# Splitting the shared expert weights earlier and running six shared units, not four, among the block projections

## Time and profile before

| what | value |
|---|---|
| median of 3 runs | 399.27 us (399.08 to 399.86) |
| the profiled execution | 399.35 us |
| its span, first to last instruction | 397.5 us |
| PE busy | 360.5 us (91%) |
| DVE busy | 310.6 us (78%) |
| POOL busy | 236.7 us (60%) |
| ACT busy | 185.4 us (47%) |

### The profile page before, as it was taken

One profiled execution on the slowest core, in us unless ns is written; L12 is line 12 of the kernel. 1 busy time (PEld: TensorE's weight loads), 2 busy tenths in 40 slices (PEclk: granted clock), 3 DMA queues, 4 the chain that ended last, 5 costly groups with the idle time before them and its releaser, 6 DMA issues.

```text
span 397.5 us, 12279 instructions
## 1 busy us (share of the span) xinstructions
PE 360.5 (91%) x4303; PEld 312.3 (79%) x4303; DVE 310.6 (78%) x846; ACT 185.4 (47%) x434; POOL 236.7 (60%) x200
## 2 busy tenths in 40 slices
PE   0166998998999999999999999999999999999993
PEld 0064675665767777777789999999999999999992
DVE  5988888978989999999967788666666666666663
ACT  2667842767344677777665444222222232222220
POOL 1555902157787773343106999188866767667676
PEclk9996999999999999999999999999999999999998
DMA  8954520001154797758663656666565555653333
GB/s 294 297 133 108 127 89 2 0 23 57 50 121 120 172 193 152 166 136 160 134 124 84 194 183 126 138 84 71 65 73 56 62 60 61 61 60 30 30 34 32
DMA packets 99157, 41.34 MB, mean 104 GB/s; under 512 B 73888, under 2 KB 92704, under 8 KB 99104
## 3 DMA queue, kind: packets, MB, share of 16 engines
q1 hardware_dynamic: 87408, 31.82, 35.0%
q0 software_dynamic: 11264, 8.69, 16.5%
q10 hardware_dynamic: 432, 0.11, 0.2%
HBM read 10.94 MB, written 12.88 MB: 60 GB/s over the span
## 4 chain that ended last, share of the span: by engine, by line
PE 81%; DVE 10%; POOL 3%; DMA 2%; issue 2%; ACT 1%; DVEq 0%; POOLq 0%; ACTq 0%
PE pY L863 18%; PE pY L696 12%; PE pAB L839 9%; PE pAB L837 9%; PE pAB L838 9%; PE pAB L684 6%; PE pAB L686 6%; PE pAB L685 6%; PE pV L708 4%; DVE hot L1201 2%; DVE hbuf L1291 1%; DMA base<-in_x 1%; POOL units L1109 1%; DMA xT<-hot 1%; POOL rows L1101 1%
## 5 line engine op out<-in xcount | busy, mean ns | idle before, releaser
L1154 POOL DMA_INDIRECT out_dram<-xT,rows x64 | 98.9, 1545 | 46.5 <-DVE xT L1653 26.6
L1145 POOL DMA_INDIRECT sorted_rows<-rows,slot x64 | 70.5, 1102 | 51.6 <-DVE hbuf L1291 38.5
L1088 ACT ACTIVATE units<-pAB 128x512 f32<-128x512 f32 x78 | 46.4, 594 | 108.9 <-PE pAB L839 93.1
L837 PE MATMUL pAB<-rows,wsp 128*128 128x128 f16 x512 | 87.6, 219 | 0.0
L838 PE MATMUL pAB<-rows,wsp 128*128 128x128 f16 x512 | 87.6, 219 | 0.0
L839 PE MATMUL pAB<-rows,wsp 128*128 128x128 f16 x512 | 87.6, 219 | 0.0
L1591 DVE SCALAR_TENSOR_TENSOR hbuf<-pAB,units 128x512 f32<-128x512 f32 x78 | 53.6, 687 | 37.6 <-PE pAB L839 37.2
L863 PE MATMUL pY<-wsp,hbuf 128*128 (+1 forms) x620 | 78.7, 279 | 0.5 <-issue 0.4
L863 PEld LDWEIGHTS pY<-wsp,hbuf 128*128 128x128 f32 x620 | 72.7, 192 | 0.8 <-issue 0.8
L696 PEld LDWEIGHTS pY<-wsp,hbuf 128*128 128x128 f32 x512 | 66.7, 191 | 8.3
L696 PE MATMUL pY<-wsp,hbuf 128*128 128x128 f32 x512 | 68.0, 276 | 0.0
(11 more groups left out here) (166 smaller groups left out, 588.4 us busy)
## 6 DMA issues: line engine op xcount, KB each, us to landing
base<-in_x SPq DMA_DIRECT2D x8, 512.0 KB, 7.4
out_dram<-base SPq DMA_DIRECT2D x16, 256.0 KB, 2.5
wraw<-in_wall SPq DMA_DIRECT2D x10, 256.0 KB, 3.1
rows<-hot SPq DMA_DIRECT2D x8, 256.0 KB, 2.7
proj<-sorted_rows SPq DMA_DIRECT2D x27, 68.5 KB, 1.9
wsp<-in_wall SPq DMA_DIRECT2D x10, 128.0 KB
sorted_rows<-rows,slot POOLq DMA_INDIRECT x64, 2.5
out_dram<-xT,rows POOLq DMA_INDIRECT x64, 3.4
```

The lines of the kernel that those rows point to most:

```text
L837: pe.matmul(o, hi, x(0), start=True, stop=False)
L1088: nc.scalar.activation(silu[:, q % 2, 0:job.cols], pAB[:, 2 * (q % 2), 0:job.cols], ACT.Silu, scale=1 / (XS * WS)).then_inc(d_silu, 1)
L1145: pool.indirect_dma_start(sorted_rows, bass.IndirectOffsetOnAxis(ap=slot[:, t:t + 1].bitcast(U32), axis=0), rows[:, t, :], None, bounds_ch ...
L1154: pool.indirect_dma_start(out_rows, bass.IndirectOffsetOnAxis(ap=meta[:, t, DEST - CW:DEST - CW + 1].bitcast(U32), axis=0), yt[:, t], None ...
```

## The change

The split of the shared weights moves to earlier steps; six units in place of four run among the projections; the units at which PE and ACT do their parts of the routing are renumbered; on DVE two calls of `shared_unit()` between routing pieces go, the column counts move behind the logit maximum, two softmax pieces are joined, one call is added behind the clip, and the attention tables move behind unit 25.

```diff
-HIGH_AT, LOW_AT = (5, 8), (8, 10)
+HIGH_AT, LOW_AT = (3, 5), (4, 6)
...
-EARLY = 4
-EARLY_AT = {6: 0, 8: 1, 10: 2, 11: 3}
-GAP_UNIT, COLUMN_UNIT, STEP_UNIT, PLACE_UNIT = 7, 10, 10, 12
-SEG_UNIT, TAB_UNIT, TABLE_UNIT, SIDES_UNIT = 15, 18, 20, 26
-LOGIT_UNIT, ABS_UNIT, WHOLE_UNIT, SIGN_UNIT = 16, 14, 19, 20
-SELECT_UNITS = (5, 6, 12, 13)
+EARLY = 6
+EARLY_AT = {4: 0, 6: 1, 8: 2, 9: 3, 11: 4, 12: 5}
+GAP_UNIT, COLUMN_UNIT, STEP_UNIT, PLACE_UNIT = 9, 11, 12, 14
+SEG_UNIT, TAB_UNIT, TABLE_UNIT, SIDES_UNIT = 17, 20, 24, 28
+LOGIT_UNIT, ABS_UNIT, WHOLE_UNIT, SIGN_UNIT = 18, 15, 20, 21
+SELECT_UNITS = (7, 8, 10, 11)
...
-                pe.wait_ge(w_split, e // 2 % 2 + 1)
+                pe.wait_ge(w_split, e // 2 % NSH + 1)
...
             ins.then_inc(paired_ready, 1)
-            shared_unit()
 
             dve.wait_ge(gap_tanh, 1)
...
-            shared_unit()
-
-            assert unit[0] == COLUMN_UNIT
-            dve.wait_ge(column_done, 1)
...
             then(v.tensor_tensor(wmax[:, 0], halves4[:, :, :, 0], halves4[:, :, :, 1], ALU.max))
             shared_unit()
 
+            assert unit[0] > COLUMN_UNIT
+            dve.wait_ge(column_done, 1)
...
+            shared_unit()
+
             idx3 = idx.rearrange("p (t k) -> p t k", k=HP)
             v.tensor_scalar(offsets, offsets, 127.5, -128.0, ALU.min, ALU.max).then_inc(clipped, 1)
             shared_unit()
 
+            shared_unit()
...
             then(v.reciprocal(quad_recip, sum_quads))
-            shared_unit()
...
+            def tables():
+
+                dve.wait_ge(table_done, 1)
...
-                if n == 0:
+                if n == 1:
+                    tables()
+                if n == 2:
                     spread_out()
-                if n == 1:
+                if n == 3:
                     extra_table()
```

More of the change, by code:

```diff
@@ L1381, in _ @@
             shared_unit()
+            assert unit[0] > COLUMN_UNIT
+            dve.wait_ge(column_done, 1)
+            v.memset(chunk_start[:, 0:1], 0.0)
+            then(v.tensor_copy(column[:], pV[:, 0, 0:CHUNKS]))
+            v.tensor_tensor(column_half[:], column[:].unsqueeze(2).broadcast_to([P, CHUNKS, 2]),
+                            c["half_mask"][:].unsqueeze(1).broadcast_to([P, CHUNKS, 2]), ALU.mult)
+            v.tensor_tensor_scan(chunk_start[:, 1:CHUNKS + 1], column[:], column[:], 0.0, ALU.add, ALU.max).then_inc(column_ready, 1)
+            shared_unit()
             idx3 = idx.rearrange("p (t k) -> p t k", k=HP)
             v.tensor_scalar(offsets, offsets, 127.5, -128.0, ALU.min, ALU.max).then_inc(clipped, 1)
+            shared_unit()
             shared_unit()
@@ L1447, in _ @@
             then(v.tensor_tensor(inverse[:, :, 1], sum_recip, by_two[:, :, 0], ALU.mult))
[L1448 to L1456, removed]
             shared_unit()
@@ L1471, in _ @@
             shared_unit()
+            def tables():
+                dve.wait_ge(table_done, 1)
+                same = c["same_gather"][:].unsqueeze(1).broadcast_to([P, 8, HI16 * GRP])
+                for k in range(2):
+                    ins = v.tensor_tensor(table[:, 4 * k:4 * k + 4].rearrange("p b s c -> p (b s) c"),
+                                          pV[:, k, :].rearrange("p (g c) -> p g c", g=8), same, ALU.mult)
+                ins.then_inc(table_ready, 1)
             def one_hot(g, u):
```

## The result

The kernel after the change took 407.01 us (median of 4 runs, 406.4 to 407.07) against 399.27 before: 7.74 us more, a ratio of 1.0184 with a 95% interval of 1.0170 to 1.0199. The forecast was 404.6, with 406.5 as the top of its range, so the result lies outside it. The direction and most of the chain of hand-overs were as forecast; the sum was 2.4 us short.

The account below looks back on a forecast made before the run. TensorE was taken to bound it (81% of the chain of waits). Routing 4.5 later plus 1.55 to the slots made 6.05, less 0.57 and 0.14 slack: 5.3; 399.27 + 5.3 = 404.6 us, range 400.8 to 406.5.

Parts of the forecast that it names:

- Part 1: Weight splits at earlier steps: DVE's halves take 1.3 and 1.6, ACT's last square root comes 2.4 us later.
- Part 2: First silu and its 1.28 table load now ahead of n(9) on ACT: n(11) 1.6 later, turn(11) at 44.1.
- the longer table load: Rival: ACT's table switch drains as long again as it loads, everything behind another 1.3 later, 405.9 us; chance 0.05.
- Part 3: Two more units between PE's projections: 9.5 from turn(11) to turn(15), routing starts at 57.7, 4.5 later.
- Part 4: Reordered routing steps on DVE: two waits go, two silu waits (1.2, 1.6) come; start to slots 1.55 longer.
- Part 5: Sort and its followers: 31st scatter lands 6.05 later, at 135.65; after slack of 0.57 and 0.14, 5.3 remains.
- Part 6: Attention tables behind unit 24: 1.28 leaves the crowded stretch; costs nothing while DVE waits for the sort, otherwise 1.2.
- VectorE alone: Rival: the sort comes sooner and VectorE alone decides, 3.05 later up to unit 24, 402.3 us; chance 0.20.
- the third sum into the base tile: Term of part 4: on DVE at unit 15, a third such sum adds 0.6 before the slots.
- Faster: Rival: added units fall into PE's waits, turn(15) not after 50.5, routing starts as before, 397.8 us; chance 0.08.
- No change: Rival: late routing start half as large, made up by units no longer behind it, no change shows; chance 0.07.

Follow-up runs that it names:

- b1: The kernel before with only the splits of the shared weights moved to their new, earlier steps 3 to 6; 401.31 us, ratio 1.0034.
- a3: The kernel after the change with the sixth early unit two steps later, behind projection 14 instead of 12; 406.76 us, ratio 1.0169.
- a6: The kernel after with one-hot stores a unit later, column counts ahead of the maximum, and five early units, not six, one more call at the end; 402.93 us.
- a2: The kernel after the change with the column counts ahead of the logit maximum again and ACT's masks at units 11 and 12; 404.77 us, ratio 1.0114.
- a1: The kernel after the change with the weighted one-hots of a batch begun one shared unit later (unit 35, not 34); 404.85 us, ratio 1.0124.
- a7: The kernel after the change with SP's fifth and later one-hot transposes held until the sort's second part has landed; 406.90 us, ratio 1.0184.
- b2: The kernel before with attention tables moved behind unit 25, side products two units later and weighted one-hots one unit later; 399.76 us, ratio 1.0005.
- a5: The kernel after the change with the splits back at their old steps and the six early units moved to suit; 405.69 us, ratio 1.0144.
- a4: The kernel after with weighted one-hots one unit later, column counts ahead of the maximum and the sixth early unit two steps later; 403.10 us, ratio 1.0075.

## Why the prediction was right in kind and short by 2.4 us

**Part 1, the splits: right.** The halves took 1.22 and 1.60, forecast 1.3 and 1.6; the root was 2.53 late, forecast 2.4. b1 shows the delay reaching the routing by itself.

**Part 2, the table load: right.** It stands at 35.59, ahead of n(9). The load took 1.28 and the silu began 0.02 behind its end, with no second load's length between. So the rival of the longer table load is out, although its 405.9 lies nearer to the result than the forecast does.

**Part 3, the units: right, 0.4 short.** Turn(11) was forecast at 44.1 and stands at 44.50; from there to turn(15) it is 9.54, forecast 9.5. The routing began 4.92 late, forecast 4.5. What a3 and a6 add is that this term is PE's amount of work: five units start the routing at 55.75, six at 57.35 with the last of them two steps later, 58.12 with it in its place.

**Part 4, the order of the routing: a term was left out.** The two new waits for silus are 1.27 and 1.54, forecast 1.2 and 1.6, and the wait at the column is gone. But start to slots grew by 2.36, not 1.55. Nearly all of the excess of 0.81 is one instruction: the maximum's second part took 1.46 instead of 0.69. The two parts in the kernel before, in DVE's order of time:

```profile
70.27 1.78 DVE L1379 TENSOR_TENSOR hot<-proj 128x1024 f32<-128x1024 f32 x1
72.09 0.69 DVE L1380 TENSOR_TENSOR work<-hot 128x512 f32<-128x512 f32 x1
```

With the column counts and a unit no longer ahead of it, the second part came to stand beside POOL's choice weights (71.86 to 74.93). I priced what the move did to waits for other engines, and not what it puts side by side. In a2, where the maximum stands later, the second part takes 0.69.

**Part 5, the sort: right in kind, 1.2 short.** The 31st scatter was issued 6.99 late. The store over its rows stood 8.51 late, behind a wait of 2.83 that a1 shows to be worth 2.2 at the end. The step that failed is "Its instructions are untouched and POOL waits for nothing else, so the 31st lands at 129.6 + 6.05" (135.65): the landing does not move along rigidly. The store that waits for it came at 138.13, 4.06 behind the issue, where the 2.5 of before was taken. Why it took longer is open; a7 shows that it takes no less with the transposes held back. What the store's lateness loses on its way was right: hf(63) is 7.76 late, 0.75 less than the store, forecast 0.71.

**Part 6, the tables: not contradicted.** Without the wait for the sort, in a1 and b2, hf(24) to hf(34) is some 0.8 longer, where 1.2 was forecast. That they cost nothing with the wait there fits the sum, but no run leaves the move out of the changed kernel.

The three terms that were short, 0.42 + 0.81 + (8.51 - 7.28), make 2.46, and the forecast of 5.3 plus these is 7.76. That it meets the 7.74 to the last digit is luck: places in one profile are not that sure.

**VectorE alone**, the rival of 402.3, asked for a sooner sort, which did not come. What it would have cost is shown by a1, the kernel without the wait for the sort: 404.85, so its price was 2.5 too low. It left out the third sum into the base tile (0.6, which part 4 had), the two overruns above (0.42 and 0.81) and the tables' cost behind unit 24 (0.75). **Faster** asked for turn(15) by 50.5; it stood at 54.04. **No change** is outside the interval.

Where the 7.7 went, then: 2.2 into the wait for the sort (a1); about 1.8 into the order of the routing (a2, by hf(24)); the rest into a start of the routing that is 4.9 late and that fewer units behind it pay back only in part. The splits alone made 0.7 to 2.0 of it in the kernel before (b1). How their share and the units' share divide in the kernel after is not settled (a5). None of the twelve runs was faster than the kernel before.

## What to carry to other kernels

Moving work of the busiest engine into an earlier gap gains only while the gap is idle: here a sixth unit pushed the next stage's start back by about as much as it gave back, and the time did not change (a4, a6), while with three or two units the other engines' pipeline held that start where it was and the missing work showed later. When a step is moved, price it by its new neighbours too, which instruction of another engine it now runs beside, as well as by the waits it loses; and do not carry a transfer's landing along as a constant (at most 2.54 became 4.06 here). Mileposts that both traces share, such as a counted product of one line, turn "7.7 us slower" into a sum by stretches in a few subtractions.

## What the runs showed of the hardware that was not expected

**A DVE operation with two inputs in SBUF, begun beside POOL arithmetic, ends nearly its own length after POOL's.** Three cases of the kernel after, from the fences above. The half at 22.44 began inside POOL's subtraction that ended at 23.11, and ended at 23.66. The half at 29.54 began inside the one that ended at 30.61, and ended at 31.14. The maximum at 74.04 began inside the pair that ended at 74.93, and ended at 75.50. That is 0.55, 0.53 and 0.57 behind, against 0.69 for either operation alone. The maximum's first part, twice as wide (1.22 for an operation of its shape alone), began beside POOL in before, after and a2, and ended 1.08 to 1.09 behind POOL's operation. So the DVE operation looks blocked until POOL is done, and not slowed in proportion. It goes the other way too: the second of POOL's pair began at 72.88, inside the maximum's first part, which ended at 74.01, and took 2.05, where the first took 1.07. The Trainium skill, SBUF — State Buffer, section "Who interferes with whom", says that a DVE instruction with two SBUF inputs contends with a GpSimd instruction that reads SBUF, and that such contention is an exclusive lock; these rows agree.

**A scatter's landing is no constant of its issue.** From the 31st issue to the store that waits for it took at most 2.54 in the kernel before, 4.06 after the change, and 4.59 with the transposes held back. In a2, a3 and a5, where a store of unit 34 waited for it too, it took 3.93 to 4.22. No run here separates the cause.
